# A graph layer's edge sums on one core: superblocks of four edge tiles in eight message slots instead of eight tiles in four slots

## The reference, cut to what matters

```python
edge_index = jnp.stack([src, dst])
h = jnp.maximum(_layernorm(x, axis=-1), 0.0)
xs = h[src]
for i in range(4):
    msgs = msgs + jnp.where((edge_type_4 == i)[:, None], xs @ W[i] + b[i], 0.0)
out = x + jax.ops.segment_sum(msgs, dst, num_segments=12500)
```

## Time and profile before

| | us |
|---|---|
| median of 3 runs | 1974.44 (1974.0 to 1974.92) |
| the profiled execution | 1970.82 |
| its span, first to last instruction | 1969.0 |
| POOL busy | 1477.7 (75%) |
| PE busy, PE weight load busy | 1119.1 (57%), 938.9 (48%) |
| DVE busy | 713.0 (36%) |
| granted TensorE clock, mean | 0.74 |

### The profile page before, as it was taken

One profiled execution on the slowest core, in us unless ns is written; L12 is line 12 of the kernel. 1 busy time (PEld: TensorE's weight loads), 2 busy tenths in 40 slices (PEclk: granted clock), 3 DMA queues, 4 the chain that ended last, 5 costly groups with the idle time before them and its releaser, 6 DMA issues.

```text
span 1969.0 us, 23372 instructions
## 1 busy us (share of the span) xinstructions
PE 1119.1 (57%) x5394; PEld 938.9 (48%) x5395; DVE 713.0 (36%) x1591; ACT 134.4 (7%) x384; POOL 1477.7 (75%) x1575
## 2 busy tenths in 40 slices
PE   6962456465464665645656556566555555555556
PEld 2322444444353444444454554455545555555555
DVE  6871233232232423424334344243333222332333
ACT  4540000000000000000000000000000000000000
POOL 7777777777777777777777777777777777777776
PEclk9985666776767767758778687787876776776867
DMA  9961222212122121212112221212312121211212
GB/s 311 317 235 50 53 53 52 53 52 53 52 53 52 52 53 52 53 52 53 52 53 53 52 53 52 53 52 53 109 52 72 52 53 52 72 52 52 72 52 62
DMA packets 94970, 144.18 MB, mean 73 GB/s; under 512 B 27065, under 2 KB 57267, under 8 KB 94947
## 3 DMA queue, kind: packets, MB, share of 16 engines
q0 software_dynamic: 50016, 102.53, 19.8%
q1 hardware_dynamic: 40537, 39.02, 5.9%
q10 hardware_dynamic: 4394, 2.40, 0.5%
HBM read 111.76 MB, written 32.09 MB: 73 GB/s over the span
## 4 chain that ended last, share of the span: by engine, by line
POOL 75%; issue 24%; PE 0%; DMA 0%; DVEq 0%; DVE 0%; POOLq 0%
POOL messages L342 69%; POOL early_x L330 6%; PE ps_sum L694 0%; DMA messages<-message_table,table_row 0%; DMA src_rows<-in_src 0%; POOLq L246 0%; DVE acc L569 0%; DVEq L229 0%; DVEq L569 0%; PE ps_i L635 0%; DVE src_col L437 0%; DVE early_f L435 0%; DVE onehot L577 0%; DVEq L595 0%; DVEq L577 0%
## 5 line engine op out<-in xcount | busy, mean ns | idle before, releaser
L342 POOL DMA_INDIRECT messages<-message_table,table_row x1443 | 1361.5, 944 | 439.8 <-issue 439.8
L694 PE MATMUL ps_sum<-messages,onehot 128*128 128x128 f32 x4438 | 843.8, 372 | 789.3 <-DMA messages<-message_table,table_row 697.9
L694 PEld LDWEIGHTS ps_sum<-messages,onehot 128*128 128x128 f32 x4438 | 796.7, 280 | 835.7 <-issue 829.0
L577 DVE SCALAR_TENSOR_TENSOR onehot<-ps_node,tile_base,dst_col 128x512 f32<-128x512 f32 x586 | 429.8, 748 | 1172.9 <-PE ps_sum L694 1086.2
L330 POOL DMA_INDIRECT early_x<-in_x,src_col x120 | 114.1, 950 | 40.9 <-issue 39.3
L649 PE MATMUL ps_y<-w_sb,h_t 128*128 128x512 f32 x196 | 104.6, 626 | 5.0 <-DVE y L505 4.7
L721 PE MATMUL ps_y<-y 128*128 128x512 f32 x240 | 106.6, 597 | 0.0
L587 DVE SCALAR_TENSOR_TENSOR y<-ps_i,tile_base,key_col 128x1024 f32<-128x1024 f32 x60 | 75.5, 1279 | 39.2 <-PE ps_y L721 39.2
L569 DVE TENSOR_TENSOR acc<-acc,ps_sum x294 | 81.4, 277 | 1.8 <-PE ps_sum L694 1.7
L420 ACT COPY bias<-ps_y 128x512 f32<-128x512 f32 x15 | 8.8, 585 | 972.4 <-PEq L725 972.4
L505 DVE TENSOR_TENSOR y<-ps_y,bias 128x512 f32<-128x512 f32 x98 | 67.0, 683 | 17.1 <-PE ps_y L649 12.1
(11 more groups left out here) (64 smaller groups left out, 139.6 us busy)
## 6 DMA issues: line engine op xcount, KB each, us to landing
message_table<-y SPq DMA_DIRECT2D x98, 256.0 KB, 3.7
messages<-message_table,table_row POOLq DMA_INDIRECT x1443, 2.5
out<-acc SPq DMA_DIRECT2D x6, 896.0 KB
acc<-in_x SPq DMA_DIRECT2D x4, 896.0 KB
early_x<-in_x,src_col POOLq DMA_INDIRECT x120
acc<-in_x ACTq DMA_DIRECT2D x2, 896.0 KB, 10.1
acc<-in_x SPq DMA_DIRECT2D x1, 832.0 KB
src_rows<-in_src SPq DMA_DIRECT2D x1, 640.0 KB
```

Of the source, the lines that this page charges most:

```text
L342: pool.indirect_dma_start(messages[:, k, t, :], None, table_rows, bass.IndirectOffsetOnAxis(ap=flat_rows[:, at + t:at + t + 1], axis=0)).t ...
L577: nc.vector.scalar_tensor_tensor(out=onehot[:, a:z, :], in0=ps_node[:, :].unsqueeze(1).broadcast_to([P, z - a, P]), scalar=tile_base[:, ba ...
L694: ins = nc.tensor.matmul(ps_sum[:, bass.ds(q % 2, 1), 0:d], onehot[:, t, :], messages[:, k, t, :], start=(t == 0), stop=(t == tiles - 1))
```

## The change

A superblock becomes four edge tiles, and the ring eight slots of four tiles, which is 32 tiles as before. There are 390 full superblocks and a last one of 3 tiles. The early superblocks become 30 of four tiles, one after every 1 × 8 = 8 table superblocks. The gathers, their number and their order are the same.

```diff
-SB_TILES = 8
-SLOTS = 4
-EARLY_SBS = 15
-EARLY_ROUNDS = 2
+SB_TILES = 4
+SLOTS = 8
+EARLY_SBS = 30
+EARLY_ROUNDS = 1
```

## The result

The changed kernel takes 2018.49 us (median of 4 runs, 2017.27 to 2020.52) against 1974.22 us of before (4 runs, 1973.92 to 1974.92): ratio 1.0225, 95% interval 1.021 to 1.024, 44 us slower. The forecast was 1994, 20 us slower, range 1972 to 2022.

The account below looks back on a forecast made before the run. POOL's gathers bound the kernel, with PE falling behind in the mixed stage. 1970.82 plus 21 of POOL's waits less 3.2 in the tail gave 1988.6; 3.6 to the median made 1992, set at 1994, range 1972 to 2022.

Parts of the forecast that it names:

- The mechanism: Mixed stage: PE's lag peaks at 52 us, over the ring's 31, so POOL waits about 21 us, not recovered.
- A single superblock at the low clock: PE, table superblock of one pair: eight passes fewer at the low clock, 3.58 us instead of 5.28.
- The early superblock: PE, mixed stage: four tiles cost 11.1 us (ends 9.1 and 13.4), where twice the tiles took 13.56 before.
- The ring: Slots between POOL and PE: POOL waits only once PE's lag is over 31 to 32 us.
- PE's round: PE, mixed stage, per 32 gathers: 38.6 us plus second pairs, against POOL's 39.95.
- The second pair: PE, superblock with two pairs: 1.8 us extra (ends 0.9 and 2.9); the handovers were worked out as 2.0.
- The -0.9 per round: PE, mixed stage: 0.9 us off each round for about one superblock, right behind the early one, at the high clock.
- The tail: After the last gather: PE is free when the rows land, a gain of 3.2 us (ends 1.5 and 3.5).
- The front: Before the first table gather: DVE's doubled range lists may take some 3 us more, but covered, so nothing.
- The ring holds: Rival: a round costs 1 us less, POOL never waits, only the tail's gain is left, 1971.2 us; chance 0.19.
- The clock stays low throughout: Rival, PE's mixed stage: 2.4 us more a round, 2045 to 2065, half of it 2020; chance 0.09.
- POOL pays for its waits: Rival: 180 more waits at up to 0.30 us stop hiding, +54 us, 2025; chance 0.04, shared with something unseen.

Follow-up runs that it names:

- e1: The changed kernel with half the ring (four slots of four tiles, 16 tiles): 2043.15 us, ratio to before 1.0351.
- e2: The changed kernel with five products of constants on PE after each table superblock: 1972.18 us, ratio to before 0.9992.
- e3: The changed kernel, where PE loads the next superblock's range before waiting for its last product, within each unrolled round: 1973.07 us, ratio to before 0.9996.
- e4: The changed kernel with early superblocks kept at eight tiles, 15 of them, one after every 16 table superblocks: 1973.13 us, ratio to before 0.9996.
- e7: The kernel before (eight tiles, four slots) with five products of constants after each table superblock: 1973.03 us, ratio to before 0.9996.
- e5: The changed kernel with only the early superblock's range loaded ahead of PE's wait for its last product: 1987.57 us, ratio to before 1.0075.
- e6: The changed kernel with ranges loaded ahead within a round and three products of constants after each table superblock: 1972.1 us, ratio to before 0.9993.
- e8: The kernel before with DVE's seven comparisons of line 547 (196 elements) done four times over: 1971.04 us, one run.

## Why the prediction was wrong in size, point by point

**The mechanism held.** The ring was used up by PE in the last third of the mixed stage, POOL waited there (the first of the sixteen waits ends at 920, the last at 1458, where 900 to 1400 was forecast) and nothing was given back. "POOL's waits list L342 behind PE's line 694 with about 20 us" was the forecast; the row names L699, where PE frees the slot, and holds 43.4 above the usual gaps. PE's wait for gathered rows fell from 697.9 to 161.1, as forecast.

**Terms that were right.** A single superblock at the low clock: 3.58 forecast, 3.60 measured. The step from the last table superblock to the early one: 3.3, and 3.25 in the mean. The early superblock: 11.1, and 11.17 in the mean of cases from 9.2 to 12.2. The ring: e1's 16 tiles fit the 20 us that were reckoned. The wait for a satisfied semaphore is free, as the earlier trace rows said.

**The step that failed is the length of PE's round**, and in it mainly two discounts for the high clock. With the forecast's prices the 29 rounds sum to 1201 us; they lasted 1223. The missing 22 us are the 22 by which POOL's waits were undervalued (43.4 instead of 21).

- *The second pair* was set at 1.8 ("some of these denser bursts will raise the clock"), though the working said 2.0. It measured 5.60 - 3.60 = 2.0, over 46 pairs 9 us.
- *The -0.9 per round*, "about one superblock a round, right behind the early one, will run at the high clock". Of the 24 one-pair superblocks right behind an early one none ran at it throughout: their passes took 1.30 to 2.07, and the gain was 0.2 per round. The high clock came elsewhere, 13 times behind a superblock of two pairs, as at 551.51 above. All one-pair superblocks together gained 18 us, 0.6 per round, where 26 had been taken off: 8 us.
- The rest is 3.60 instead of 3.58 for a single one (4 us) and the step to and through the early superblock (1 us).

So the discount was nearer in size than in place, which was luck. The kernel before could have warned: of ten one-pair superblocks right behind an early one, two took 2.05 for their 16 passes, the others 2.68 to 3.78. The sentence that the result is steep ("0.5 us more or less per round is 15 us") was right: 0.8 per round was the whole miss. It should have kept me from taking two discounts on the clock that no row of thin bursts showed.

The prediction read the Trainium skill (TensorE: Matmul & The Clock Gate, "HAM oscillation — how this bites in real kernels") as speaking of this change. That section tells of groups of matmuls that are shorter than the waits between them. Here a burst of 2.07 was longer than its gap of 1.50, so the section doesn't cover the case, and the trace shows the low clock all the same, in 140 of 162.

**The tail** was forecast at -3.2 and is -0.9. Part is a slip: a two-pair superblock with the gap behind it is 3.6 + 2.0, as my own terms say, not 4.1. These are the rows that answer to the earlier trace rows:

```profile
2004.82 4.11 PE L694 MATMUL ps_sum<-messages,onehot 128*128 128x128 f32 x16 [2.31 <-DMA messages<-message_table,table_row]
...
2010.54 1.65 PE L694 MATMUL ps_sum<-messages,onehot 128*128 128x128 f32 x6 [1.61 <-DVE acc L569]
2012.49 0.29 DVE L569 TENSOR_TENSOR acc<-acc,ps_sum  x1 [2.54 <-PE ps_sum L694]
```

From 2004.82 to 2010.54 it is 5.72 where before it was 7.27, and the last six passes run at the low clock (1.65 instead of 0.93).

**The front** was forecast at nothing and is 0.7. POOL's first need of a slot was indeed covered; the 0.7 is in the gathers of the first stage (last section).

**The rivals.** "The ring holds" failed in the changed kernel, and came true with each of e2, e3 and e4. "The clock stays low throughout" was nearer than its chance of 0.09: half of it was priced at 2020, and the result is 2018. That it meets the result is in part luck: its price for L721 didn't come, since the early superblock does reach the high clock midway (1.00 in 1124 to 1130.5), and 0.6 of the 0.9 was gained after all. "POOL pays for its waits" is out by e2, which has the same waits and none of the time. The register load's floor of about 0.6 us, which the Trainium skill gives (DMA: Bandwidth & Descriptors, "Latency and other measured facts"), would not have helped: the 1.50 holds the load already. The trace agrees in size: e3 takes 0.73 out of the gap by moving the load.

## What to carry to other kernels

Slack of an engine is to be read for the stretch in which its work is densest, and as a rate against the supply: here 1 us per round of 40 was 30 us of time, because the ring lends only once. Smaller pieces pay the fixed part of each piece twice, and on PE also the clock: count short bursts at the low level unless a row shows the same density at the high one. When an engine is late by a few per cent, filling its idle time with products of constants, or moving its register load ahead of its drain, were here each worth the whole loss (e2, e3); where the engine isn't late, e7 shows nothing for it.

## What the runs showed of the hardware that I had not expected

**More work on PE made PE faster.** e2 adds ten passes to every table superblock and shortens it from 3.60 to 2.66.

**The mean duration of POOL's gathers differs between executions by 0.2%.** It takes two levels: 1361.3 to 1361.6 us busy over the 1443 gathers in the profiled executions of before, e1, e2, e3, e5, e6 and e8 (943 or 944 ns each), and 1364.0 to 1364.7 in the changed kernel, e4 and e7 (945 or 946 ns). This is about 3 us. In e4 and e7 the profiled execution took what the median did (1973.05 and 1973.13; 1973.03 both), in before, e2, e3 and e6 it was 2.6 to 3.6 us faster than the median. That fits the 3.6 of before, which I could only note; what sets the level isn't shown. Differences under 0.2% between single executions of this kernel say nothing of a change.

**Some DVE operations stretch POOL's gathers.** In the first stage of the changed kernel, while DVE ran the seven comparisons of line 547, now with 391 elements:

```profile
136.46 5.35 DVE L547 SCALAR_TENSOR_TENSOR y<-ranges,order 1x391 f32<-1x391 int32 x7 [0.87 <-DMA ranges<-ranges_by_chunk]
```

```profile
137.41 1.41 POOL L330 DMA_INDIRECT early_x<-in_x,src_col  x1 [0.30 <-issue]
139.13 1.21 POOL L330 DMA_INDIRECT early_x<-in_x,src_col  x1 [0.30 <-issue]
140.64 1.19 POOL L330 DMA_INDIRECT early_x<-in_x,src_col  x1 [0.30 <-issue]
142.13 0.95 POOL L330 DMA_INDIRECT early_x<-in_x,src_col  x1 [0.30 <-issue]
```

Three gathers are longer by 0.46, 0.26 and 0.24, and the next, beside DVE's reduction, is normal again. It repeats: in all seven kernels with 391 elements (the changed one and e1 to e6) three or four gathers beside these comparisons take 1.19 to 1.47, and their first table gather starts at 158.5 to 159.2. With seven comparisons of 196 elements the longest gather takes 1.06 (before) or 1.01 (e7), and the first table gather starts at 158.2 or 157.7. The Trainium skill (GPSIMD Engine Reference, "1. Specifications") says that the SBUF interface of GpSimd is shared with VectorE and contended by DVE instructions with two SBUF inputs, which line 547 has. The trace agrees in where the gathers stretch; that this sharing is the cause isn't shown. In e8 four times as many comparisons of 196 elements stretched one gather by 0.25 and two by 0.05, so the length of one operation, not the number, would have to matter. That wasn't tried further, and the 0.7 us stay attributed by place alone, 0.1 of them to a first gather of the first stage that started later (4.67 against 4.54).
